# A group norm and a shifted depthwise convolution: shorter tile heads, narrower frame copies, another order around the variances

## The chip, the cores and the metric

The kernel runs on one core of a Trainium2 chip. The metric is the device time in microseconds from launch to end. An x tensor of 201 MB is read once from HBM and an output of the same size is written once.

## What is computed

`x` is (16, 768, 64, 64) in fp32. It is normalized in 32 groups of 24 channels over all pixels, per image. Each of the 48 blocks of 16 channels is then shifted by a whole number of pixels (about a multiple of 16 in each direction, up to 48), filtered with a separable 3x3 Gaussian whose centre is off by the fraction of the offset, and added to `x`:

```python
g = v.reshape(B_, G, C_ // G, H_, W_)
m = jnp.mean(g, axis=(2, 3, 4), keepdims=True)
s = jnp.var(g, axis=(2, 3, 4), keepdims=True)
gn = ((g - m) / jnp.sqrt(s + eps)).reshape(v.shape)
...
off_int = lax.stop_gradient(jnp.round(offset * SCALE)); sub = off_px - off_int
shifted = gn shifted by off_int, zero outside the image
kern = jnp.exp(-(kx * kx + ky * ky) / (2.0 * SIGMA * SIGMA)); kern = kern / kern.sum(axis=(1, 2), keepdims=True)
x = x + depthwise 3x3 convolution of shifted with kern
```

A shift of 16, 32 or 48 pixels leaves only a window of about 50, 34 or 18 rows or columns that isn't zero.

## The kernel before

**Tiles and units.** A tile is one position of the offset grid for 8 images: 16 channels x 8 images on 128 partitions, 4096 pixels each (2 MB). There are 96 tiles. Three tiles make a unit, which holds two whole groups (48 channels), so statistics are ready unit by unit: 32 units. Units go in pairs from the list `PAIRS`: an even unit is called large here (more window), an odd one small. Tiles live in `xs`, a ring of 10 slots, and are changed in place.

**SyncE** alone issues DMAs. `store(n)` waits for VectorE to be done with tile n; a load into a slot waits for the store of the tile that had it. Loads are woven in between stores in the order `EARLY` and `AGAIN`, and one waiting DMA holds back those behind it.

**TensorE** forms the group sums: 8 chunks of 512 a tile against a 0/1 matrix (in fp32 each is two passes, so 16 records a tile), all into `sum_ps` (L289). Then come `means(u + 1)` (L304 to L306), which spread ScalarE's reduced sum to the partitions, and `variances(u)` (L346 to L354), which do so with the squares. In a large unit the order is: sums of two tiles of the next unit, variances, sums of the third, means. In a small unit it is: sums of all three, variances, means. PE rows of L289 with "bands" are the first or third tile of a unit, with "halves" the second.

**ScalarE** does `sum_means` (L463), the means (L470), the squares (L484, about 3.7 us each), the variance with its scale (L492), and `fill_frame` (L417): it copies the rows of the tile that are needed, less the mean, over their whole 64 columns into the padded `frame`. There is one frame, so a copy waits for the second operation (L709) of the tile before. `fill_frame` reads a word from `fills` and picks one of four copies by the number of rows (64, 50, 34 or 18).

**GpSimd** turns the variances into the row weights `col_w`: one power for the unit (L253), then for each tile L257, L260 and L266.

**VectorE** first works out all per-tile numbers in a chain of small operations (L600 to L669), sums one tile (L677), and then runs a loop with one pass for each tile (L751, `tile_of`). A pass takes four words (kind, where to, where from, and the column of its weights) that a register load (L708) brought in during the pass before; works out registers (L727, L732); goes down four branches of `choose` (L185, L187) to one of 16 forms of `smooth_tile`, by 4 row and 4 column sizes; and issues five operations: L704 (centre and nearer neighbour in the row), L709 (the other neighbour), L713, L716 and L719 (the rows, added to x). L713 waits for `col_w`. Each operation waits for the one before it in its instruction; a gap between them of 0.04 us is what that costs.

Sizes of a tile are rows x columns, so L704 "128x3200" is a window of 50 x 64 or 64 x 50.

## Time and profile before

| | |
|---|---|
| median of 3 runs | 973.79 us (973.67 to 978.83) |
| the profiled execution | 979.06 us, its span 977.1 us |
| TensorE matmuls | 785.6 us busy, 80% |
| VectorE | 824.8 us, 84% |
| ScalarE | 638.9 us, 65% |
| GpSimd | 368.1 us, 38% |
| DMA | 98.0% of 16 engines' time in the main queue; 403.09 MB, mean 413 GB/s |
| granted TensorE clock | 0.888 |

The profile's page comes from one execution. Busy shares are means over the span. Its second part cuts the span into 40 slices of 24.4 us and gives the DMA rate of each. A group row of an engine ends with the idle time before its instructions and what ended most of it; "issue" means that nothing that the profile shows was waited for. Sequencer work (DVEq, ACTq: registers, branches) isn't counted as busy.

### The profile page before, as it was taken

Reading aid. Unit: us, or ns where it says so; the run is one execution under the profiler, and the core shown is the slowest. Engines: PE = TensorE matmul, PEld = TensorE weight load, DVE = VectorE, ACT = ScalarE, POOL = GpSimd, SP = SyncE. Lnnn points to the kernel's source line nnn. Section 1 sums busy time; section 2 is a strip of 40 time slices with the busy share of each in tenths; the row PEclk is TensorE's granted clock in tenths of the full one; section 3 lists DMA queues with packets and bytes.
Section 4 is the critical chain, followed back from the end, with each engine's and each line's share of the span. In section 5 each row is a group of like instructions: output and inputs, shape, how many; then the busy total and the mean of one; then the engine's idle time right before and its main releaser. Section 6 shows DMA issues by size and latency. Waiting matters only on the chain.

```text
span 977.1 us, 9088 instructions
## 1 busy us (share of the span) xinstructions
PE 785.6 (80%) x2132; PEld 383.6 (39%) x2132; DVE 824.8 (84%) x551; ACT 638.9 (65%) x461; POOL 368.1 (38%) x348
## 2 busy tenths in 40 slices
PE   0998987979979698897979879689797997979820
PEld 0544443434434343353434434345343443434410
DVE  7587988777798997978889899898998979797795
ACT  7778676564766747678466746577675785774661
POOL 0214034340432624013254393463845438250312
PEclk9999988989979799897998979989898897989955
DMA  9999999999999999999999999999999999999948
GB/s 364 427 401 423 392 405 429 429 429 428 430 429 430 432 428 414 430 429 430 431 429 406 398 433 376 407 419 393 431 408 430 430 427 431 431 431 430 430 208 343
DMA packets 27821, 403.09 MB, mean 413 GB/s; under 512 B 3216, under 2 KB 3216, under 8 KB 3216
## 3 DMA queue, kind: packets, MB, share of 16 engines
q1 hardware_dynamic: 27792, 402.71, 98.0%
q8 instruction: 17, 0.28, 0.1%
q14 instruction: 12, 0.10, 0.0%
HBM read 201.38 MB, written 201.33 MB: 412 GB/s over the span
## 4 chain that ended last, share of the span: by engine, by line
DVE 28%; DMA 27%; PE 20%; POOL 7%; issue 7%; ACT 5%; DVEq 3%; ACTq 2%; SPq 0%; POOLq 0%
PE sum_ps L289 17%; DMA out_dram<-xs 15%; DMA xs<-x_dram 12%; DVE xs L713 6%; DVE xs L716 6%; DVE smooth L709 6%; DVE smooth L704 6%; DVE xs L719 4%; POOL small L253 2%; POOL small L260 2%; ACT frame L417 2%; POOL small L257 2%; ACT unused L484 2%; POOL small L266 1%; ACTq L393 1%
## 5 line engine op out<-in xcount | busy, mean ns | idle before, releaser
L289 PE MATMUL sum_ps<-xs,bands 128*128 128x512 f32 x976 | 483.5, 653 | 51.2 <-DMA xs<-x_dram 51.2
L484 ACT ACTIVATE unused<-xs,small 128x4096 bf16 (+1 forms) x94 | 348.3, 3706 | 8.3 <-ACT small L470 4.8
L417 ACT ACTIVATE frame<-xs,small (+1 forms) x96 | 223.3, 2326 | 184.3 <-DVE smooth L709 183.3
L289 PEld LDWEIGHTS sum_ps<-xs,bands 128*128 128x128 f32 x976 | 200.6, 210 | 295.4 <-issue 282.2
L253 POOL TENSOR_TENSOR small<-small 128x3 f32<-128x3 f32 x32 | 41.6, 1299 | 570.6 <-ACT small L492 570.6
L289 PE MATMUL sum_ps<-xs,halves 128*128 128x512 f32 x496 | 230.0, 619 | 17.4 <-DMA xs<-x_dram 17.4
L704 DVE SCALAR_TENSOR_TENSOR smooth<-frame,side_w 128x612 f32 (+5 forms) x96 | 163.6, 1705 | 72.2 <-ACT frame L417 37.1
L713 DVE SCALAR_TENSOR_TENSOR xs<-smooth,small,xs 128x612 f32 (+5 forms) x96 | 163.5, 1703 | 51.9 <-POOL small L266 49.6
L709 DVE SCALAR_TENSOR_TENSOR smooth<-frame,side_w,smooth x96 | 159.7, 1664 | 7.5 <-DVE smooth L704 4.1
L719 DVE SCALAR_TENSOR_TENSOR xs<-smooth,small,xs 128x594 f32 (+9 forms) x96 | 159.8, 1664 | 3.4
L716 DVE SCALAR_TENSOR_TENSOR xs<-smooth,small,xs 128x594 f32 (+9 forms) x96 | 159.7, 1664 | 3.4
L289 PEld LDWEIGHTS sum_ps<-xs,halves 128*128 128x128 f32 x496 | 97.4, 199 | 146.4 <-issue 119.3
L266 POOL TENSOR_SCALAR small<-xs,small 128x3 f32<-128x3 f32 x96 | 119.5, 1245 | 9.5
L260 POOL TENSOR_SCALAR small<-small 128x1 f32<-128x1 f32 x96 | 106.6, 1110 | 8.4
L257 POOL TENSOR_SCALAR small<-small 128x1 f32<-128x1 f32 x96 | 99.7, 1039 | 3.3
L463 ACT ACTIVATE sum_ps<-sum_ps 128x512 f32<-128x512 f32 x31 | 18.0, 581 | 73.8 <-PE sum_ps L289 71.0
L304 PE MATMUL mean_ps<-small,halves 128*128 128x1 f32 x62 | 13.0, 279 | 61.6 <-ACT sum_ps L463 61.6
L304 PEld LDWEIGHTS mean_ps<-small,halves 128*128 128x128 f32 x62 | 10.7, 217 | 74.3 <-ACT sum_ps L463 74.3
L470 ACT ACTIVATE small<-mean_ps 128x3 f32<-128x3 f32 x31 | 5.4, 175 | 27.6 <-PE mean_ps L306 27.6
L492 ACT ACTIVATE small<-var_ps,small 128x3 f32<-128x3 f32 x32 | 8.2, 255 | 22.6 <-PE var_ps L354 21.7
L346 PEld LDWEIGHTS var_ps<-small,bands 128*128 128x128 f32 x62 | 11.9, 194 | 18.8 <-issue 18.8
L484 ACT ACTIVATION_READ_ACCUMULATOR unused<-xs,small 128x1 f32 x94 | 17.5, 186 | 0.0
(132 smaller groups left out, 259.3 us busy)
## 6 DMA issues: line engine op xcount, KB each, us to landing
xs<-x_dram SPq DMA_DIRECT2D x96, 2048.0 KB, 14.8
out_dram<-xs SPq DMA_DIRECT2D x96, 2048.0 KB, 17.7
smooth<-offset_dram SPq DMA_DIRECT2D x1, 48.0 KB, 4.1
```

Source lines behind the costliest of these rows:

```text
L253: V.tensor_tensor(rstd0, var, power, ALU.pow).then_inc(rstd_step, 1)
L257: V.tensor_scalar(fix[:, column], var[:, column], rstd0[:, column], rstd0[:, column], ALU.mult, ALU.mult).then_inc(rstd_step, 1)
L260: V.tensor_scalar(rstd[:, column], fix[:, column], -0.5, 1.5, ALU.mult, ALU.add).then_inc(rstd_step, 1)
L266: V.tensor_scalar(col_w[:, now * UT + i, :], base_w[:, position, :], rstd0[:, column], rstd[:, column], ALU.mult, ALU.mult).then_inc(col_w ...
L289: last = nc.tensor.matmul(sum_ps[:, :], (FIRST, SAME, SECOND)[i], slot_px(n, c * BANK, (c + 1) * BANK), start=(i == 0 and c == 0), stop=(i ...
L417: nc.scalar.activation(frame[:, bass.ds(b, rows * PITCH)].rearrange("p (r c) -> p r c", c=PITCH)[:, :, LEFT:LEFT + W], xs[:, bass.ds(a, ro ...
L484: nc.scalar.activation(unused[:, :], xs[:, bass.ds(n % SLOTS * PIX, PIX)], ACT.Square, bias=neg_mean[:, i:i + 1], accum_out=squares[:, i:i ...
L704: V.scalar_tensor_tensor(sm, frame_window(beside, cols), side_w[0][:, bass.ds(n, 1)], frame_window(src, cols), ALU.mult, ALU.add).wait_op( ...
L709: V.scalar_tensor_tensor(part, frame_window(behind, cols - 1), side_w[1][:, bass.ds(n, 1)], part, ALU.mult, ALU.add).wait_op(half_smooth, ...
L713: V.scalar_tensor_tensor(x_window(0, rows), sm, col_flat[:, bass.ds(weights + 1, 1)], x_window(0, rows), ALU.mult, ALU.add).wait_op(smooth ...
L716: V.scalar_tensor_tensor(x_window(1, rows), sm[:, 0:rows - 1], col_flat[:, bass.ds(weights, 1)], x_window(1, rows), ALU.mult, ALU.add).wai ...
L719: V.scalar_tensor_tensor(x_window(0, rows - 1), sm[:, 1:rows], col_flat[:, bass.ds(weights + 2, 1)], x_window(0, rows - 1), ALU.mult, ALU. ...
```

## The change

- A tile keeps four words, but the fourth is now the address of the nearer neighbour (`BESIDE`), worked out at setup; the column of the weights comes from the tile's number instead. `col_w` is laid out by kernel row first and tile second, and `side_w` has a column ahead, so that the count 1 to 96 indexes both. The loop runs over that count. The parity and the address `behind` are worked out in the form itself, after the first operation.
- The load of the next tile's words goes from behind the first operation to behind the second.
- `fill_frame` has six copies: the four as before, and two of 34 columns (64 or 34 rows) for tiles of 34 or 18 columns. Its word also holds a column. The words for it move into partitions 64 to 127 of `words`.
- In small units TensorE forms the variances after two tiles' sums, as in large ones. ScalarE takes the variance before `sum_means`.
- Setup has 14 more small operations on VectorE, and GpSimd six memsets fewer.

```diff
-    KIND, TO, FROM, COLUMN = range(WORDS)
+    KIND, TO, FROM, BESIDE = range(WORDS)
     ROW_BITS = (H - SIDES[-1]).bit_length()
+    NARROW = 2
+    COPIES = [(rows, W) for rows in SIDES] + [(SIDES[k], SIDES[NARROW]) for k in (0, NARROW)]
+    COL_BITS = (W - SIDES[NARROW]).bit_length()
...
+        col_w = sb("col_w", [P, 3, 2 * UT])
...
+        side_w = [sb(f"side_w{k}", [P, TILES + 1]) for k in range(2)]
         words = sb("words", [P, WORDS * (TILES + 1)], i32)
-        fills = sb("fills", [P, TILES], i32)
+        fills = words[HALF:P, 0:TILES]
...
-                    V.tensor_scalar(col_w[:, now * UT + i, :], base_w[:, position, :], rstd0[:, column],
+                    V.tensor_scalar(col_w[:, :, (now * UT + i + 1) % (2 * UT)], base_w[:, position, :], rstd0[:, column],
...
-                    early = UT if u % 2 else UT - 1
-                    sums(u + 1, range(early))
+                    sums(u + 1, range(UT - 1))
                     variances(u)
-                    sums(u + 1, range(early, UT))
+                    sums(u + 1, range(UT - 1, UT))
...
-                word = act.snap(entry, min_val=0, max_val=(len(SIDES) << ROW_BITS) - 1)
-                row = word & (1 << ROW_BITS) - 1
-                rows_kind = act.snap(word >> ROW_BITS)
+                word = act.snap(entry, min_val=0, max_val=(len(COPIES) << ROW_BITS + COL_BITS) - 1)
+                column = word & (1 << COL_BITS) - 1
+                row = (word >> COL_BITS) & (1 << ROW_BITS) - 1
+                copy_kind = act.snap(word >> ROW_BITS + COL_BITS)
                 base = act.snap(slot, min_val=0, max_val=(SLOTS - 1) * PIX)
                 first = isinstance(u, int) and u == 0 and i == 0
                 act.reg_mov(frames, u * UT + i)
-                act.reg_mov(copy_from, base + row * W)
-                act.reg_mov(copy_to, row * PITCH + PAD * PITCH)
+                act.reg_mov(copy_from, base + row * W + column)
+                act.reg_mov(copy_to, row * PITCH + column + PAD * PITCH)
+                source = act.snap(copy_from, min_val=0, max_val=SLOTS * PIX)
+                target = act.snap(copy_to, min_val=PAD * PITCH, max_val=FRAME_ROWS * PITCH)
+                done = act.snap(frames, min_val=1, max_val=TILES)
                 if i == 0:
                     act.wait_ge(fill_mean_ready, u + 1)
                 def emit(k):
-                    rows = SIDES[k]
-                    a = act.snap(copy_from, min_val=0, max_val=(SLOTS - 1) * PIX + (H - rows) * W)
-                    b = act.snap(copy_to, min_val=PAD * PITCH, max_val=(PAD + H - rows) * PITCH)
+                    rows, cols = COPIES[k]
+                    a = source.with_bounds(min_val=0, max_val=(SLOTS - 1) * PIX + (H - rows) * W + W - cols)
+                    b = target.with_bounds(min_val=PAD * PITCH, max_val=(PAD + H - rows) * PITCH + W - cols)
                     if not first:
-                        act.wait_ge(smooth_ready, act.snap(frames, min_val=1, max_val=TILES))
+                        act.wait_ge(smooth_ready, done)
                     nc.scalar.activation(
-                        frame[:, bass.ds(b, rows * PITCH)].rearrange("p (r c) -> p r c", c=PITCH)[:, :, LEFT:LEFT + W],
-                        xs[:, bass.ds(a, rows * W)].rearrange("p (r c) -> p r c", c=W),
+                        frame[:, bass.ds(b, rows * PITCH)].rearrange("p (r c) -> p r c", c=PITCH)[:, :, LEFT:LEFT + cols],
+                        xs[:, bass.ds(a, rows * W)].rearrange("p (r c) -> p r c", c=W)[:, :, 0:cols],
                         ACT.Identity, bias=fill_mean[:, i:i + 1]).then_inc(frame_ready, 1)
-                choose(act, rows_kind, 0, len(SIDES), emit)
+                choose(act, copy_kind, 0, len(COPIES), emit)
...
+                variances(u, first)
                 if ahead and not large:
                     sum_means(u + 1)
-                variances(u, first)
...
+            narrow, low, half = positive[:, :, 0], positive[:, :, 1], whole[:, :, 0]
+            chained(V.tensor_scalar(narrow, kind[:, :, 0], float(NARROW), None, ALU.is_ge))
+            chained(V.tensor_scalar(low, kind[:, :, 1], float(NARROW), float(len(SIDES)), ALU.is_ge, ALU.add))
+            chained(V.tensor_tensor(low, low, kind[:, :, 1], ALU.subtract))
+            chained(V.tensor_tensor(low, low, narrow, ALU.mult))
+            chained(V.tensor_tensor(low, low, kind[:, :, 1], ALU.add))
+            chained(V.tensor_scalar(half, kind[:, :, 1], float(NARROW), float(H - SIDES[NARROW]), ALU.is_ge, ALU.mult))
+            chained(V.tensor_scalar(half, half, float(H), None, ALU.subtract))
+            chained(V.tensor_tensor(half, half, narrow, ALU.mult))
+            chained(V.scalar_tensor_tensor(half, half, float(H), first_row[:, :, 1], ALU.add, ALU.min))
+            chained(V.scalar_tensor_tensor(code[:, :, 0], low, float(1 << ROW_BITS), half, ALU.mult, ALU.add))
+            chained(V.tensor_tensor(narrow, narrow, left, ALU.mult))
+            chained(V.tensor_scalar(narrow, narrow, float(W - SIDES[NARROW]), None, ALU.mult))
+            chained(V.scalar_tensor_tensor(code[:, :, 0], code[:, :, 0], float(1 << COL_BITS), narrow,
...
+            chained(V.tensor_tensor(code[:, :, 0], code[:, :, 0], side, ALU.subtract))
+            chained(V.tensor_scalar(by_tile(word_of[:, :, BESIDE]), for_halves(code[0:HALF, :, 0]),
...
                 dve.wait_ge(frame_ready, done)
-                V.scalar_tensor_tensor(sm, frame_window(beside, cols), side_w[0][:, bass.ds(n, 1)], frame_window(src, cols),
+                V.scalar_tensor_tensor(sm, frame_window(beside, cols), side_w[0][:, bass.ds(done, 1)], frame_window(src, cols),
                                        ALU.mult, ALU.add
                                        ).wait_op(tile_done, done_count, "sem-ge").then_inc(half_smooth, 1)
-                dve.reg_load(next_tile, words[0:1, bass.ds(done * WORDS, WORDS)])
-                V.scalar_tensor_tensor(part, frame_window(behind, cols - 1), side_w[1][:, bass.ds(n, 1)], part,
+                turn = kind_of % 2
+                behind = (src + 1 - turn).with_bounds(min_val=1, max_val=most + 1)
+                part = smooth[:, bass.ds(turn.with_bounds(min_val=0, max_val=1), rows * cols)].rearrange(
+                    "p (r c) -> p r c", c=cols)[:, :, 0:cols - 1]
+                V.scalar_tensor_tensor(part, frame_window(behind, cols - 1), side_w[1][:, bass.ds(done, 1)], part,
                                        ALU.mult, ALU.add
                                        ).wait_op(half_smooth, done_count, "sem-ge").then_inc(smooth_ready, 1)
+                dve.reg_load(next_tile, words[0:1, bass.ds(done * WORDS, WORDS)])
                 dve.wait_ge(col_w_ready, done)
-                V.scalar_tensor_tensor(x_window(0, rows), sm, col_flat[:, bass.ds(weights + 1, 1)], x_window(0, rows),
+                V.scalar_tensor_tensor(x_window(0, rows), sm, col_w[:, 0, bass.ds(done % (2 * UT), 1)], x_window(0, rows),
...
-            def tile_of(n):
-                dve.reg_mov(done_count, n + 1)
-                done = dve.snap(done_count, min_val=1, max_val=TILES)
+            def tile_of(done):
+                dve.reg_mov(done_count, done)
                 kind_of = dve.snap(next_tile[KIND], min_val=0, max_val=2 * len(SIDES) ** 2 - 1)
-                dve.reg_mov(at_turn, kind_of & 1)
-                turn = dve.snap(at_turn, min_val=0, max_val=1)
                 dst = dve.snap(next_tile[TO], min_val=0, max_val=SLOTS * PIX)
                 src = dve.snap(next_tile[FROM], min_val=1, max_val=FRAME_ROWS * PITCH)
-                dve.reg_mov(at_behind, src + 1 - turn)
-                dve.reg_mov(at_beside, src + 2 * turn - 1)
-                beside = dve.snap(at_beside, min_val=0, max_val=FRAME_ROWS * PITCH)
-                behind = dve.snap(at_behind, min_val=0, max_val=FRAME_ROWS * PITCH)
-                weights = dve.snap(next_tile[COLUMN], min_val=0, max_val=(2 * UT - 1) * 3)
+                beside = dve.snap(next_tile[BESIDE], min_val=0, max_val=FRAME_ROWS * PITCH)
...
-            with dve.Fori(0, TILES) as n:
+            with dve.Fori(1, TILES + 1) as n:
...
```

## Rows read from the trace of the kernel before

**Rows 1.** The page, part 2: DMA rate in 40 slices.
```profile
GB/s 364 427 401 423 392 405 429 429 429 428 430 429 430 432 428 414 430 429 430 431 429 406 398 433 376 407 419 393 431 408 430 430 427 431 431 431 430 430 208 343
```

**Rows 2.** Busy by stretch: PE, PEld, DVE, ACT, POOL (instructions), PEclk, DMA share, GB/s.
```profile
57.00:132.00 75.00, 67.30 (x196) 32.66 (x194) 65.37 (x41) 56.93 (x41) 22.86 (x30) 0.98 0.99 398
132.00:360.00 228.00, 194.34 (x517) 92.82 (x517) 191.18 (x113) 142.57 (x107) 75.94 (x70) 0.89 1.01 429
360.00:384.00 24.00, 21.46 (x63) 10.74 (x64) 18.33 (x18) 18.41 (x14) 9.31 (x12) 0.88 1.01 414
...
528.00:690.00 162.00, 137.16 (x374) 67.31 (x373) 147.24 (x83) 102.31 (x76) 78.94 (x52) 0.89 0.98 403
690.00:744.00 54.00, 44.33 (x124) 21.98 (x123) 49.23 (x29) 37.72 (x27) 30.15 (x19) 0.91 1.01 421
...
924.00:977.00 53.00, 9.18 (x31) 6.12 (x29) 40.43 (x28) 18.70 (x16) 15.54 (x16) 0.57 0.68 289
```

**Rows 3.** VectorE's timeline (start, length, instruction, idle before): tiles 48, 54, 60, 66, 72.
```profile
501.03 3.55 DVE L704 SCALAR_TENSOR_TENSOR smooth<-frame,side_w 128x3200 f32 x1 [0.92 <-DVE xs L719]
...
564.28 3.55 DVE L704 SCALAR_TENSOR_TENSOR smooth<-frame,side_w 128x3200 f32 x1 [0.95 <-DVE xs L719]
...
627.26 3.59 DVE L704 SCALAR_TENSOR_TENSOR smooth<-frame,side_w 128x3200 f32 x1 [0.94 <-DVE xs L719]
...
686.70 3.56 DVE L704 SCALAR_TENSOR_TENSOR smooth<-frame,side_w 128x3200 f32 x1 [1.48 <-ACT frame L417]
...
746.66 3.55 DVE L704 SCALAR_TENSOR_TENSOR smooth<-frame,side_w 128x3200 f32 x1 [1.48 <-ACT frame L417]
```

**Rows 4.** Waits of VectorE: line, releaser, us in all, times, longest.
```profile
DVE xs L713 <- POOL small L266: 49.6, 32, 5.5
DVE smooth L704 <- ACT frame L417: 37.1, 24, 5.5
...
DVE smooth L704 <- issue: 14.8, 13, 1.5
```

**Rows 5.** Chain of waits at tile 94's head (start, us, what; DVEq is the sequencer).
```profile
959.42 0.22 DVEq L727
...
959.68 0.17 DVEq L732
...
960.61 0.93 DVEq L708
```

**Rows 6.** VectorE's timeline: first operation of tile 52, third of tile 63.
```profile
549.43 1.16 DVE L704 SCALAR_TENSOR_TENSOR smooth<-frame,side_w 128x900 f32 x1 [1.18 <-issue]
...
669.20 1.42 DVE L713 SCALAR_TENSOR_TENSOR xs<-smooth,small,xs 128x1152 f32 x1 [0.67 <-POOL small L266]
```

**Rows 7.** Frame copies: ScalarE's groups by shape, and tile 52's on the timeline.
```profile
L417 ACT ACTIVATE frame<-xs,small 128x4096 f32 x12 | 45.0, 3747 | 29.8 <-DVE smooth L709 29.8
...
545.44 1.27 ACT L417 ACTIVATE frame<-xs,small  x1 [0.77 <-DVE smooth L709]
```

**Rows 8.** Timeline, unit 17: second sums, last square, the means on ScalarE.
```profile
523.35 7.03 PE L289 MATMUL sum_ps<-xs,halves 128*128 128x512 f32 x16
...
528.52 3.71 ACT L484 ACTIVATE unused<-xs,small 128x4096 bf16 x1
...
540.52 0.18 ACT L470 ACTIVATE small<-mean_ps 128x3 f32<-128x3 f32 x1 [0.83 <-PE mean_ps L306]
```

**Rows 9.** VectorE's timeline in the setup.
```profile
13.61 0.21 DVE L639 CAST fills<-smooth 128x96 int32<-128x96 f32 x1
13.86 0.21 DVE L642 SCALAR_TENSOR_TENSOR smooth<-smooth 128x48 f32<-128x48 f32 x1
...
20.33 4.42 DVE L677 TENSOR_REDUCE small<-xs 128x1 f32<-128x4096 f32 x1 [1.11 <-DMA xs<-x_dram]
```

**Rows 10.** GpSimd's timeline beside tile 48's first operation.
```profile
500.97 3.67 POOL L257 TENSOR_SCALAR small<-small 128x1 f32<-128x1 f32 x1
```

**Rows 11.** The tail: TensorE's sums of tile 94, VectorE's start of tile 95.
```profile
911.20 8.67 PE L289 MATMUL sum_ps<-xs,halves 128*128 128x512 f32 x16 [2.69 <-DMA xs<-x_dram]
...
966.19 0.56 DVE L704 SCALAR_TENSOR_TENSOR smooth<-frame,side_w 128x324 f32 x1 [1.04 <-issue]
```

**Rows 12.** TensorE's timeline: a tile's sums after an idle time.
```profile
276.94 10.04 PE L289 MATMUL sum_ps<-xs,bands 128*128 128x512 f32 x16 [6.23 <-DMA xs<-x_dram]
```

61 lines of the change are left out of this document (27 added, 34 removed).

## The prediction

> **What bounds the kernel now.** I read the page first, then the busy time by stretch, then the waits of VectorE, then the chain and the timelines around the places that these named.
>
> The page shows a DMA-bound kernel with dents. The rate stands at 427 to 433 GB/s in most of the 40 slices and falls in a few: early, around slices 22 to 29, and at the end [rows 1]. By stretches, 132 to 360 us runs at 429 GB/s and is full. I take 430 as full speed. A lost microsecond of DMA there is lost for good, since the queue is full before and after. The losses, as length times (1 - rate/430): 57 to 132 us 5.6 us, 360 to 384 us 0.9 us, 528 to 690 us 10.2 us, 690 to 744 us 1.1 us [rows 2]. The last stretch, 924 to 977 us, is the tail: all loads are in, and VectorE works off what is left.
>
> So two things can shorten the span: the 11.3 us lost in the middle (528 to 744), and the tail. In the middle VectorE sets the pace. A pair of units is 6 tiles and so 12 transfers of 2.097 MB, 58.5 us at 430 GB/s. The first operations of tiles 48, 54, 60, 66 and 72 start at 501.03, 564.28, 627.26, 686.70 and 746.66 [rows 3], so the pairs take 63.25, 62.98, 59.44 and 59.96 us: 4.7, 4.5, 0.9 and 1.4 over 58.5, together 11.5. That is the 11.3 us lost, measured a second way. VectorE's own work cannot shrink (no operation on data changes), only the idle time between its operations. That idle time is 49.6 us for row weights from GpSimd and, before a tile's first operation, 14.8 us "issue" and 37.1 us for the frame copy on ScalarE [rows 4].
>
> **The change part by part.**
>
> *Short heads.* Ahead of a tile's first operation VectorE's sequencer runs the loop's end, a block at L727 (0.22 us), one at L732 (0.17 us), and four branches [rows 5]. While the tile before is short, this isn't covered: tile 52 starts after 1.18 us of idle with "issue" as releaser, and nothing else was late [rows 6]. The change takes the parity, both derived addresses, the weights column and the n+1 out of the head. What is left is a move of the count and four names for loaded registers. The L732 block goes whole, and of L727 most: 0.17 + 0.22 and the three gaps of some 0.03 between them make 0.48; one short block stays. I take 0.43 a head. Bounds: 0 (the register work is only renamed) and 1.0 (branches get shorter too). Heads behind a tile of long operations are covered and give nothing.
>
> *The moved register load* (L708, 0.93 us [rows 5]) goes from behind the first operation to behind the second. It stalls a small tile as much in the one place as in the other, so 0. But the frame is released by the second operation, so ScalarE can copy the next one 0.2 to 0.4 us sooner after tiles of 612 elements or fewer. Parity and `behind` are now worked out during the first operation, and `done % 6` during the others: they hide behind 0.56 us at the least (0; 0.3 a small tile if not).
>
> *Narrow copies.* A frame copy of 4096 elements takes 3747 ns, one of 1152 takes 1.27 us [rows 7], so about 0.84 ns an element. Tiles with 34 or 18 columns now copy 2176 in place of 4096 or 3200 (1.6 and 0.9 us less), or 1156 in place of 2176 (0.85 less). It shortens the path only where VectorE waits for the frame. In the middle it isn't: tile 52's frame is complete at 546.7, 2.7 us before the tile starts [rows 6, 7], and the row of a large unit's first tile that does name the frame as its releaser (686.70, tile 66 [rows 3]) is of 50 columns and isn't narrowed. There it gives 0. Where it does shorten a wait, before 460 us, DMA is full and the time isn't lost now.
>
> *Variances ahead of the third tile's sums, in small (odd) units.* Before, TensorE ran 3 x 16 matmuls of the next unit, 7.03 us a tile, and then the variances. Now they come up to one tile, 7 us, sooner, and ScalarE turns them over before the means. The wait for row weights at the first tile of a small unit then goes: 0.67 us at tile 63 and again at 69 [rows 6]. At tiles 51 and 57 it is 0.40, where the variance still has to pass the frame copy on ScalarE and four GpSimd operations: I take half, 0.2. Behind the moved variances stand the third tile's sums and the next means, and behind those the squares and the frames of the small unit. The variances take 1.5 us of TensorE and no longer run beside ScalarE's sum (0.6 us), so where TensorE is late the means come about 1 us later. In unit 17 the variances would wait for the last square, which ends at 532.2; the second sums end at 530.1. So: wait 2, variance tail 0.5, third sums 7.0, ScalarE 0.7, means 0.8, makes 541, less VectorE's own lead, 540.3; before, the means came at 540.52 [rows 8]. No loss, no gain.
>
> *Setup.* 14 more chained operations on VectorE at about 0.24 us each (the spacing of L639 and L642: 13.61 and 13.86) are 3.4 us, of which 1.1 is covered by the wait of L677 for its load [rows 9]. The first unit starts 2.2 us later. Up to 57 us the DMA queue is fed by the ten first loads, so that is covered; behind it the store of tile 3 loses its margin, since it had only some 3 us of queue ahead. I charge 0.5 us. Bounds: 0 and 2.2.
>
> *GpSimd against VectorE.* GpSimd's one-element operation took 3.67 us beside a VectorE operation of 3.55 [rows 10]: it gets through at the seams. The idle heads are such seams, and they are now half as wide. The rows bound the cost: nothing, or one more of its short operations behind each large unit's second VectorE operation, some 0.35 us. I take 0 and put 0.35 a pair in the range.
> The Trainium skill (SBUF — State Buffer, "Who interferes with whom") says that a DVE instruction with two SBUF inputs holds the shared read port against a GpSimd instruction that reads SBUF, for the whole instruction. The trace agrees with that at 3.67 us. By that rule shorter heads do cost the 0.35 a pair, and the sum below would be 1.4 us less.
>
> **The sum, in the profiled run.** Up to tile 46 both kernels meet the DMA-bound chain (load, sums, means, square, frame), so nothing carries over. From there:
> - Lead at tile 48: its head and the one before, 0.8. Pair 48 to 53: heads of 52, 53 and 54, 1.3, and 0.2 of weights: 1.5. New excess 4.7 - 0.8 - 1.5 = 2.4.
> - Pair 54 to 59: the same, 4.5 - 1.5 = 3.0.
> - Pair 60 to 65: three heads 1.3, the weights 0.67, earlier release 0.2: 0.9 - 2.2 = below zero.
> - Pair 66 to 71: 1.4 - 2.4, below zero too.
> So 5.4 us are still lost in place of 11.3: gain 5.9. The dent at 360 to 384 (0.9) comes from the same lateness of tile 32, which leads by 0.7: half, 0.4. Tail: its start hangs on the load that TensorE takes at 911.20, and in the last large unit the order is as before; then the heads of 91, 94 and 95 (0.25 and twice 0.43; tile 95's shows 1.04 us of "issue") [rows 11]: 1.1. In all 5.9 + 0.4 + 1.1 - 0.5 = 6.9 us.
>
> The profiled execution took 979.06 us, its span 977.1; the median of the three runs is 973.79, 5.3 below it, so either it was a slow one or the profile costs something. I take the gain off the median: **966.9 us**.
>
> **The rivals.**
> 1. *Nothing in the middle.* Something else sits just under the heads: the frame after the square (545.44 for tile 52, four microseconds ahead of its use), or the weights. Then only the tail's 1.1 and the 0.67s count: 972.5. Against it: "issue" is the last releaser of these heads [rows 6]. Chance 0.18.
> 2. *The heads don't shrink.* Copies of registers stay, or six copy kinds and longer leaves bring later code. Then 0.2 to 0.67 a pair from the weights, less the setup: 973.3. Chance 0.08.
> 3. *The middle is mended whole.* A head loses 0.9: four a pair make 3.6, and 63.25 - 0.8 - 3.8 is at 58.5. Then 11.3 + 0.9 + 2.0 - 0.5 go: 960.1. Chance 0.12.
> 4. *Slower: TensorE now waits for squares.* Place: variances of units 17, 19, 21 and 23, ahead of the third sums. The sums after an idle TensorE took 10.04 us in place of 7.03 [rows 8, 12]. If the new wait brings that about, the means come 3 us later; the square and the frame of tile 52 have 0.8 us of slack, so VectorE starts 2.2 us later in each of four pairs and in the two that follow. The middle loses 5.4 + 4 x 2.2 + 2 x 1 = 16 in place of 11.3 and the start 2.2: with the tail's 1.1 off, 979.6. It decides from about 1 us of delay of the means. Against it: the wait in unit 17 is only 2 us, and TensorE had just worked for 16 us. Chance 0.10.
> The Trainium skill (TensorE: Matmul & The Clock Gate, Part 1) has the array fall to 1.2 GHz after an idle time and return to 2.4 only under work. The granted clock of 0.57 in the tail [rows 2] and the 10.04 us agree. It is the rule that speaks for rival 4.
>
> **How the numbers follow.** Forecast 0.52 at 966.9; the rivals 0.18, 0.08, 0.12 and 0.10. The forecast's own bounds: heads 0.25 to 0.7, ports 0 to 1.4, start 0 to 2.2, give 962.5 to 971. The range takes in rivals 1 and 2 and stops near rival 3: 960.5 to 974.5. About 0.5% (4.9 us) is what a measurement can tell from no change, so "faster" is below 968.9: 0.38 of the forecast's and 0.12 of rival 3's chance, 0.50. Slower, above 978.7: 0.09. The rest, 0.41, is the same.
>
> **What would show each step.** The idle time before tile 52's first operation falls from 1.18 to about 0.75 us; the L732 block is gone. The frame copies of 4096 elements fall from 12 to 4 (the tiles of 50 columns). The wait for row weights falls below 30 us from 49.6. The rate in 528 to 690 us rises from 403 to about 415 GB/s, and first operations of tiles 48, 54 and 60 stand 61 to 62 us apart. TensorE shows a gap of about 2 us ahead of the variances in unit 17. The prediction is wrong if the heads are as wide as before, if the sums after the variances take 9 us or more, or if tile 52 waits for its frame.

## The result and the profile after

| | before | after |
|---|---|---|
| median, 20 runs each, in turns | 977.11 us (973.67 to 979.31) | 972.45 us (970.14 to 976.21) |
| ratio after/before | | 0.9961, 95% interval 0.9951 to 0.9972 |
| profiled execution, its span | 979.06, 977.1 us | 973.67, 971.6 us |
| GpSimd busy | 368.1 us | 436.9 us |
| frame copies, mean of 96 | 2326 ns | 1909 ns |

The change gains 3.8 us by the ratio (2.7 to 4.8), 4.7 by the medians. The forecast was 966.9, a gain of 6.9. The time lies inside the range (960.5 to 974.5), and the outcome is within 0.5% of no change, to which I gave 0.41. The direction was right, the size wasn't. The forecast missed the median by 5.5 us: 3.3 of them are the median that it started from (973.79 where the twenty runs give 977.11), 2.2 the gain.

The page of the kernel after, DMA rate in 40 slices, where [rows 1] has that of before:

```profile
GB/s 361 429 396 396 401 400 431 429 428 430 429 432 430 428 430 429 431 427 431 428 429 428 405 431 407 411 430 409 430 431 431 431 431 430 431 431 428 424 206 346
```

Counted from 1, the dents of slices 16 and 22 (414, 406) are gone (429, 428), and slices 25, 26, 28 and 30 (376, 407, 393, 408) read 407, 411, 409 and 431. But the early ones, 3 to 6, are worse on the whole: 396, 396, 401, 400 where there were 401, 423, 392, 405.

Busy by stretch of the kernel after (PE, PEld, DVE, ACT, POOL with instructions, then granted clock, DMA share, GB/s), beside [rows 2]:

```profile
57.00:132.00 75.00, 70.22 (x201) 33.75 (x199) 67.90 (x42) 53.12 (x41) 36.72 (x30) 0.98 0.99 391
132.00:360.00 228.00, 190.43 (x518) 91.18 (x519) 191.68 (x113) 136.14 (x106) 93.74 (x72) 0.92 1.01 429
360.00:384.00 24.00, 21.03 (x60) 10.05 (x59) 18.84 (x18) 16.89 (x15) 10.38 (x13) 0.92 1.01 431
528.00:690.00 162.00, 137.57 (x379) 66.06 (x377) 151.68 (x85) 98.53 (x77) 90.25 (x56) 0.94 1.00 417
690.00:744.00 54.00, 46.09 (x128) 22.50 (x129) 50.66 (x30) 33.18 (x25) 31.47 (x17) 0.91 1.01 430
```

By the measure of the prediction, length times (1 - rate/430): 528 to 690 loses 4.9 us in place of 10.2, 690 to 744 nothing in place of 1.1, 360 to 384 nothing in place of 0.9. So 7.3 us are gained, and 57 to 132 loses 6.8 in place of 5.6.

Waits of VectorE in the kernel after (line, releaser, us in all, times, longest), beside [rows 4]:

```profile
DVE smooth L727 <- ACT frame L423: 69.3, 30, 6.9
DVE xs L740 <- POOL col_w L270: 29.2, 26, 5.2
DVE smooth L727 <- DVE xs L746: 11.0, 27, 0.6
DVE xs L740 <- DVE smooth L734: 5.4, 12, 1.0
```

(L727, L734, L740, L743 and L746 are the five operations that were L704, L709, L713, L716 and L719.) "issue" is gone as a releaser. The wait for row weights fell by 20.4 us, and the wait for the frame rose by 32.2.

VectorE's timeline in the kernel after at tiles 52, 54, 60 and 63, beside [rows 3, 6]:

```profile
546.97 1.16 DVE L727 SCALAR_TENSOR_TENSOR smooth<-frame,side_w 128x900 f32 x1 [0.64 <-ACT frame L423]
...
560.75 3.55 DVE L727 SCALAR_TENSOR_TENSOR smooth<-frame,side_w 128x3200 f32 x1 [0.41 <-DVE xs L746]
...
622.12 3.55 DVE L727 SCALAR_TENSOR_TENSOR smooth<-frame,side_w 128x3200 f32 x1 [0.41 <-DVE xs L746]
...
663.63 1.42 DVE L740 SCALAR_TENSOR_TENSOR xs<-smooth,col_w,xs 128x1152 f32 x1 [0.45 <-POOL col_w L270]
```

Heads (the idle time before a tile's first operation) of 1.18, 0.95 and 0.94 us are 0.64, 0.41 and 0.41 us long: 0.54 less each. Tile 48 starts at 499.37, so the first two pairs take 61.38 and 61.37 us where they took 63.25 and 62.98.

**A ledger of the queue.** To compare executions I counted, for each kernel, when the main DMA queue had finished its k-th transfer of 2 MB, less k times 4.865 us (what one takes when the queue is full). The rise of that figure between two points is DMA time lost there.

```
transfers done (at about)     before  before, again  after
25  (126 us)                  10.7    9.1            12.4
101 (496 us)                  13.2    12.5           14.2
106 (520 us)                  13.3    12.5           14.2
146 (715 us)                  25.3    23.0           19.7
185 (905 us)                  26.0    23.6           20.6
192 (the end)                 41.9    39.5           36.5
```

Middle (106 to 146): 12.0 and 10.5 before, 5.5 after. Up to 25 transfers the kernel after loses 1.7 us more than the first execution of the kernel before and 3.3 more than the second. From 185 transfers to the end the figure rises by 15.9 us in all three, so by this measure the tail is no shorter. The second column is a second execution of the kernel before, which the experiments below brought.

### The profile page after: what moved, and what is told of

It is laid out like the page before. It is cut to its first block, busy times and chain, and to the rows that moved or that the text cites. A ratio compares the mean times of both kernels' runs of the same rounds, so it can differ in the third digit from the quotient of the medians.

```text
span 971.6 us, 9186 instructions
## 1 busy us (share of the span) xinstructions
PE 776.9 (80%) x2132; PEld 375.9 (39%) x2132; DVE 827.7 (85%) x565; ACT 598.0 (62%) x461; POOL 436.9 (45%) x342
## 4 chain that ended last, share of the span: by engine, by line
DMA 36%; DVE 29%; PE 15%; POOL 7%; issue 5%; ACT 3%; ACTq 2%; DVEq 1%; SPq 0%; POOLq 0%
DMA out_dram<-xs 21%; DMA xs<-x_dram 14%; PE sum_ps L293 13%; DVE xs L740 7%; DVE xs L743 6%; DVE xs L746 5%; DVE smooth L727 5%; DVE smooth L734 4%; POOL small L261 3%; POOL small L264 2%; POOL small L257 2%; ACT frame L423 1%; ACT unused L490 1%; ACTq L395 1%; POOL col_w L270 1%
## 5 line engine op out<-in xcount | busy, mean ns | idle before, releaser
L423 ACT ACTIVATE frame<-xs,small (+1 forms) x96 | 183.3, 1909 | 178.6 <-DVE smooth L734 176.1
L257 POOL TENSOR_TENSOR small<-small 128x3 f32<-128x3 f32 x32 | 51.6, 1612 | 497.2 <-ACT small L498 497.2
L293 PE MATMUL sum_ps<-xs,halves 128*128 128x512 f32 x496 | 221.8, 600 | 21.5 <-DMA xs<-x_dram 21.5
L727 DVE SCALAR_TENSOR_TENSOR smooth<-frame,side_w 128x612 f32 (+5 forms) x96 | 163.6, 1704 | 82.1 <-ACT frame L423 69.3
L740 DVE SCALAR_TENSOR_TENSOR xs<-smooth,col_w,xs 128x612 f32 (+5 forms) x96 | 163.6, 1704 | 37.5 <-POOL col_w L270 29.2
L734 DVE SCALAR_TENSOR_TENSOR smooth<-frame,side_w,smooth x96 | 159.8, 1665 | 3.4
L743 DVE SCALAR_TENSOR_TENSOR xs<-smooth,col_w,xs 128x594 f32 (+9 forms) x96 | 159.8, 1665 | 3.4
L746 DVE SCALAR_TENSOR_TENSOR xs<-smooth,col_w,xs 128x594 f32 (+9 forms) x96 | 159.8, 1664 | 3.4
L293 PEld LDWEIGHTS sum_ps<-xs,halves 128*128 128x128 f32 x496 | 94.0, 192 | 146.5 <-issue 113.2
L264 POOL TENSOR_SCALAR small<-small 128x1 f32<-128x1 f32 x96 | 134.3, 1399 | 8.4
L270 POOL TENSOR_SCALAR col_w<-xs,small 128x3 f32<-128x3 f32 x96 | 126.1, 1313 | 9.5
L261 POOL TENSOR_SCALAR small<-small 128x1 f32<-128x1 f32 x96 | 124.4, 1296 | 3.3
```

The costliest lines, as they stand in the source:

```text
L257: V.tensor_tensor(rstd0, var, power, ALU.pow).then_inc(rstd_step, 1)
L261: V.tensor_scalar(fix[:, column], var[:, column], rstd0[:, column], rstd0[:, column], ALU.mult, ALU.mult).then_inc(rstd_step, 1)
L264: V.tensor_scalar(rstd[:, column], fix[:, column], -0.5, 1.5, ALU.mult, ALU.add).then_inc(rstd_step, 1)
L270: V.tensor_scalar(col_w[:, :, (now * UT + i + 1) % (2 * UT)], base_w[:, position, :], rstd0[:, column], rstd[:, column], ALU.mult, ALU.mul ...
L293: last = nc.tensor.matmul(sum_ps[:, :], (FIRST, SAME, SECOND)[i], slot_px(n, c * BANK, (c + 1) * BANK), start=(i == 0 and c == 0), stop=(i ...
L423: nc.scalar.activation(frame[:, bass.ds(b, rows * PITCH)].rearrange("p (r c) -> p r c", c=PITCH)[:, :, LEFT:LEFT + cols], xs[:, bass.ds(a, ...
```

## The experiments

Each time is a median, and each ratio is to the kernel before, run beside it. That had 976.13 us beside the first four experiments; 976.35 beside the kernel before again, nine moves, 14 setup operations and the shorter chain; 977.11 beside four moves, the old heads, 42 setup operations and the last one.

**Heads alone.** The kernel after, with copies of 64 columns and the old order put back, so that mainly what concerns VectorE's heads is left of the change. Twelve of the 14 setup operations go with the narrow copies (not shown in this excerpt), and the first tile starts at 30.57 us, as before the change, where the kernel after has 32.58.

```diff
-    COPIES = [(rows, W) for rows in SIDES] + [(SIDES[k], SIDES[NARROW]) for k in (0, NARROW)]
-    COL_BITS = (W - SIDES[NARROW]).bit_length()
+    COPIES = [(rows, W) for rows in SIDES]
+    COL_BITS = 0
...
-                    sums(u + 1, range(UT - 1))
+                    early = UT if u % 2 else UT - 1
+                    sums(u + 1, range(early))
```

> The kernel before with the short heads and the four words alone: all copies are 64 columns wide and the variances of small units stay behind the third sums. Theory A (the heads carry the gain): heads such as tile 52's fall from 1.18 to 0.64 us, pairs of units in 501 to 690 us take about 61.5 us of VectorE's time, the middle loses 5 to 7 us of DMA in place of 12, and the time is 4 to 6 us below before (971 to 973 where before is 977). Theory B (the new order carries it, heads hit another wait): the middle still loses 10 us or more, time within 2 us of before.

972.84 us, ratio 0.996 (0.9945 to 0.9974): the gain of the whole change. The middle loses 7.2 us by the ledger, a little over what theory A had.

**Order alone.** The kernel before with the new order on TensorE and ScalarE.

```diff
-                    early = UT if u % 2 else UT - 1
-                    sums(u + 1, range(early))
+                    sums(u + 1, range(UT - 1))
                     variances(u)
-                    sums(u + 1, range(early, UT))
+                    sums(u + 1, range(UT - 1, UT))
...
+                variances(u, first)
                 if ahead and not large:
                     sum_means(u + 1)
-                variances(u, first)
```

> The kernel before with only the order around the variances changed in small units, on TensorE and ScalarE. Theory A: waits for row weights at the first tile of a small unit fall, but the second tile waits for its frame in their place, since the means come about 1 us later; the middle keeps 10 to 12 us of loss; time within 1.5 us of before. Theory B: the time falls by 3 us or more.

977.52 us, ratio 1.002 (1.0006 to 1.0034): it gains nothing, and costs 2.0 us (0.6 to 3.3). VectorE's waits in this run:

```profile
DVE smooth L702 <- ACT frame L416: 66.1, 30, 7.3
DVE xs L711 <- POOL small L266: 19.5, 22, 5.1
```

The waits for weights fell from 49.6 to 19.5 us, those for the frame rose from 37.1 to 66.1 [rows 4]. Together they are 85.6 us in place of 86.7: the order renames the wait. In the program's new order the means, on which the squares and the frames of a small unit hang, stand behind the variances.

**Old order in the kernel after** (the two edits above, backwards).

> The changed kernel with the order around the variances put back. Theory A: within 1.5 us of the changed kernel (972), either way; if the order costs, it is by the frames of tiles 4, 76, 82 and 88, which wait up to 6.9 us. Theory B: back near before, 976 to 977.

972.77 us, ratio 0.9962 (0.9948 to 0.9976), like the kernel after. Against heads alone this adds the narrow copies and the twelve setup operations that work out their words: 972.84 and 972.77. The two together bring nothing. Each by itself isn't separated: if the operations cost here what they cost in the kernel before (below), the copies would have gained as much, and no run tells.

**The weights table later in the setup.** In the kernel after, VectorE's sum of its own tile comes before the chain that works out the row weights' table.

```diff
+            dve.wait_ge(loaded[UT - 1], 16)
+            V.tensor_reduce(own_sum, slot_px(UT - 1), mybir.AxisListType.X, ALU.add).then_inc(vector_sum_ready, 1)
...
             dve.wait_ge(exps_ready, 1)
             chained(V.tensor_tensor(norm[:, :, :], e[:, 0], e[:, 1], ALU.add))
```

> The changed kernel; on VectorE the last part of the setup (norms, side weights, base weights; some 3.4 us) now runs behind the sum of the third tile instead of ahead of it. Theory A (the longer setup costs 1.7 us at the start, seen as lost DMA up to 126 us): L677's successor starts at about 20.3 again, the loss up to 126 us falls from 12.4 to about 10.5, time 1.5 to 2 us below the changed kernel: about 970.5. Rival: the loss there is one of SyncE's order of stores and loads and isn't moved by VectorE; time as the changed kernel's.

972.88 us, ratio 0.9959 (0.9944 to 0.9974): no gain shown. VectorE's first tile starts at 30.51 in place of 32.58 and 57 to 90 us runs at 400 GB/s in place of 384 (1.2 us), but 90 to 132 us at 389 in place of 397 (0.8 us the other way). I had expected 1.5 to 2 us; an interval 3 us wide doesn't rule out 1.2, but there is no sign of them.

**The kernel before again.**

> The kernel before, unchanged, profiled a second time: it prices the spread of a single execution, which my sums were read from. My theory: part of what missed in the size is that the gain read from one profiled execution (span 977.1, a long one) was taken off a median of three that lay below the twenty runs that followed (973.79 against 977.11). Then the ratio is 1.000 with its interval around it, the span of this profile may lie anywhere from 973 to 978, and the middle (528 to 690 us) again runs at 401 to 408 GB/s, with tiles 48, 54 and 60 62.7 to 63.4 us apart. The rival: the execution that I read was of the usual kind, in which case the span is 976.5 to 977.5 again and the stretches agree within 1 GB/s.

976.78 us, ratio 1.0006 (0.9991 to 1.002), span 974.7. Stretches 57 to 132 and 528 to 690:

```profile
57.00:132.00 75.00, 67.19 (x196) 32.66 (x194) 64.86 (x40) 57.98 (x42) 25.53 (x30) 0.98 1.00 408
...
528.00:690.00 162.00, 140.57 (x373) 68.14 (x371) 147.01 (x84) 100.12 (x74) 81.27 (x53) 0.88 0.99 407
```

The same program: 408 against 398 GB/s in the one stretch and 407 against 403 in the other [rows 2]. The execution that I read was 2.4 us longer than this one, of which 1.5 in the middle, while the median from which I took the gain was the lowest of all: 973.79 of 3 runs against 976.1 to 977.1 of 17 to 25. The first theory holds.

**Longer heads, nine moves.** The kernel before with

```diff
                 dve.reg_mov(done_count, n + 1)
+                for k in range(9):
+                    dve.reg_mov(at_turn, n + k + 2)
```

> The kernel before with nine more moves of a register in the head of a tile. Theory (heads carry the gain): each head behind a short tile grows by about 0.5 us (an estimate from the block of L732, 0.17 us for about three register instructions), tile 52's from 1.18 to about 1.7, and the time goes the other way by as much as the short heads brought, some 4 to 6 us: 980.5 to 982.5 beside 976.5, ratio 1.004 to 1.006. Stretch 528 to 690 falls from 403 to about 392 GB/s. Rival (the time is set by the rest of the tile loop or by fixed things, and heads_only gained by something else, such as fewer instructions to fetch): ratio within 1.001 of the kernel before.

993.64 us, ratio 1.0182 (1.0162 to 1.0202). The direction holds, the size doesn't: 17.3 us, three times what I expected. Tile 52's head, the waits, and the stretches that lost most:

```profile
554.22 1.16 DVE L704 SCALAR_TENSOR_TENSOR smooth<-frame,side_w 128x900 f32 x1 [1.80 <-issue]
```
```profile
DVE smooth L704 <- issue: 91.7, 53, 6.7
DVE xs L713 <- POOL small L266: 18.2, 18, 4.3
```
```profile
360.00:384.00 24.00, 20.93 (x52) 9.82 (x51) 18.37 (x17) 17.46 (x11) 9.17 (x9) 0.86 0.96 377
384.00:528.00 144.00, 121.67 (x307) 57.66 (x306) 124.07 (x67) 94.39 (x65) 58.40 (x50) 0.87 1.01 423
528.00:690.00 162.00, 134.47 (x365) 66.63 (x363) 143.37 (x79) 100.59 (x73) 76.63 (x51) 0.87 0.96 393
690.00:744.00 54.00, 46.03 (x116) 22.46 (x117) 48.00 (x25) 35.42 (x25) 32.38 (x19) 0.84 0.98 399
```

The head is 0.62 us longer, much as the short ones are shorter, and it is about so in the other tiles whose head was open before (tile 53 from 1.01 to 1.64, tile 69 from 0.66 to 1.28). Only tile 0 starts 1.2 us later (31.72 against 30.48). That speaks against stalls at some tiles as the cause. But now stretches lose that were full: 384 to 528 us runs at 423 GB/s (2.3 us lost), 690 to 744 loses 3.9 in place of 1.1. "issue" is the releaser of 53 heads in place of 13.

**Longer heads, four moves** (as above, `range(4)`).

> The kernel before with four more moves in the head in place of nine: tile 52's head should go from 1.18 to about 1.45 us (0.61 for nine moves makes 0.07 a move). Heads 0.54 shorter brought 3.5 to 4.5 us, heads 0.61 longer cost 17.3. Theory (thresholds: a pair of units loses DMA time only for what it is over 58.5 us, and each lengthening brings more pairs over): the cost of this step lies between, and below half of 17.3: about 6 us, 982 to 983, ratio 1.005 to 1.007. Rival (something else comes with nine moves, such as a fetch of instructions that no longer fits, and heads cost in proportion): less than 3 us, or nearly the whole 17.

981.31 us, ratio 1.0045 (1.003 to 1.0061): 4.2 us, a little under the 6 of the theory, and a quarter of the price of nine moves; tile 52's head is 1.48 us. With heads alone, and the kernel before as the zero, there are four points: 0.54 us shorter, 3.9 us gained; 0.30 longer, 4.2 lost; 0.62 longer, 17.3 lost. In proportion to four moves, nine would cost 8.7. So the cost grows faster than the heads, and of the rival's two prices neither came.

The thresholds are one reason: the pairs from tiles 42, 72 and 78 took 58.73, 58.04 and 58.20 us before, 58.93, 58.58 and 59.03 with four moves and 59.81, 59.53 and 58.99 with nine, so pairs that had been near or under 58.5 went over it. The waits are another, which I hadn't named. In this run

```profile
DVE xs L713 <- POOL small L266: 32.8, 23, 6.9
```

where there were 49.6 us: when a tile starts later, it waits less for its row weights. At tiles 48, 51, 54, 57 and 60 that wait was 0.39 to 0.67 us and is gone with four moves. The pair from tile 48 went from 63.25 to 63.42 us with four moves and to 64.92 with nine. How much of the 17.3 us each of the two makes isn't separated.

**The old heads in the kernel after.**

```diff
+                for k in range(8):
+                    dve.reg_mov(done_count, done + k + 1)
                 dve.reg_mov(done_count, done)
```

> The changed kernel with eight moves in the head, which gives back the 0.54 us that its heads had lost (tile 52's head from 0.64 to about 1.18), and leaves the narrow copies, the new order and the setup. Theory (the short heads carry the whole gain, narrow copies and order nothing): the time of the kernel before or 1 to 2 us over it, 976.5 to 978.5, ratio 1.000 to 1.002, stretch 528 to 690 us at 402 to 408 GB/s. Rival (order and narrow copies bring a part on their own): 973 to 975.

977.59 us, ratio 1.0009 (0.9996 to 1.0022), 528 to 690 us at 407 GB/s:

```profile
547.29 1.16 DVE L727 SCALAR_TENSOR_TENSOR smooth<-frame,side_w 128x900 f32 x1 [1.20 <-issue]
```

With the heads at 1.20 us again, the rest of the change leaves the time of the kernel before. Shown from both sides (this run and heads alone): the short heads carry the gain. Order, narrow copies and longer setup come to about nothing together.

**A longer setup.** The kernel before with 14, and then with 42 more chained operations ahead of the weights table:

```diff
+            for _ in range(14):
+                chained(V.tensor_scalar(code[:, :, 0], code[:, :, 0], 1.0, None, ALU.mult))
             dve.wait_ge(exps_ready, 1)
```

> The kernel before with 14 more chained one-column operations in VectorE's setup, which is what the change adds there by my count. My prediction charged 0.5 us with bounds of 0 and 2.2; the ledger of the kernel after against before showed 1.7 us more DMA loss by 126 us. If the setup is the cause of that: the ledger at 126 us rises by 1 to 2 us over the run of the kernel before of this call, and the time by the same, 977.5 to 978.5. Rival (that 1.7 us was the spread of single executions, and the first ten loads cover the setup): the time is within 0.5 us of the kernel before.

> The kernel before with 42 more chained operations in the setup, three times the dose of the run with 14, which came out 2.1 us slower (0.4 to 3.3). At 0.24 us each they are 10.1 us. Theory (the setup lies on the path, of which only about 1 us is covered): 976.4 plus 8 to 9 us, 984 to 986, with the ledger of the DMA queue up by as much by 126 us. Rival (the first ten loads cover the setup and the 2.1 us were spread): up to 978.5.

978.41 us, ratio 1.0019 (1.0004 to 1.0034), and 983.19 us, ratio 1.0064 (1.0048 to 1.008): 2.1 us by the medians (0.4 to 3.3 by the ratio) for 3.4 us of operations and 6.1 (4.7 to 7.8) for 10.1, so some 0.6 us a microsecond; for the large dose I had expected 8 to 9. VectorE's first tile starts at 32.65 and 38.86 where it started at 30.55. Stretch 57 to 90 us, with no more operations, 14 and 42:

```profile
57.00:90.00 33.00, 30.83 (x96) 15.60 (x95) 28.28 (x20) 26.74 (x20) 8.71 (x11) 0.97 0.99 405
```
```profile
57.00:90.00 33.00, 30.82 (x96) 15.43 (x94) 29.08 (x19) 27.50 (x21) 7.95 (x10) 0.99 0.95 376
```
```profile
57.00:90.00 33.00, 33.00 (x93) 15.83 (x92) 29.28 (x18) 27.62 (x19) 7.94 (x10) 1.00 0.79 321
```

The ledger at ten transfers (53.5 us) is 4.8 to 4.9 us in all of them, so the first loads cover the setup up to there, as predicted. Behind them 405, 376 and 321 GB/s are 1.9, 4.1 and 8.4 us lost. Up to 126 us the small dose no longer stands out: its ledger has 10.6 us there, where the two executions of the kernel before have 10.7 and 9.1, and the large dose has 15.9. So the price of 14 operations rests on the times of the runs, that of 42 on the queue as well.

**A shorter chain on GpSimd.** The kernel after, with the power and one multiplication a tile.

```diff
-                    V.tensor_scalar(fix[:, column], var[:, column], rstd0[:, column], rstd0[:, column],
-                                    ALU.mult, ALU.mult).then_inc(rstd_step, 1)
...
-                    V.tensor_scalar(rstd[:, column], fix[:, column], -0.5, 1.5,
-                                    ALU.mult, ALU.add).then_inc(rstd_step, 1)
...
-                                    rstd[:, column], ALU.mult, ALU.mult).then_inc(col_w_ready, 1)
+                                    None, ALU.mult).then_inc(col_w_ready, 1)
```

> The changed kernel with a shorter chain on GpSimd: the power and then one multiplication a tile. It leaves out the refinement step of the reciprocal root. Theory: in the kernel after, GpSimd finds narrower seams between VectorE's operations, and so the third operation of each large unit's first tile waits 0.72 to 1.17 us for its row weights where it waited 0.39 to 0.67. That is a cost of the short heads that my sum took at nothing. With a third of the GpSimd operations these waits go to 0 to 0.2: in the middle 4 x 0.7 = 2.8 us of VectorE's time, of which the stretch from 528 to 690 us can give back 2 to 2.8, and in the tail the sums of the last but one unit are followed by VectorE's third operation 1 to 2 us sooner. Together 3 to 4.5 us below the kernel after: 968 to 969.5, ratio 0.991 to 0.993 to the kernel before, stretch 528 to 690 us at 422 to 425 GB/s. Rival (the frames or the heads are late next, so the waits only change their name): 971.5 to 973, ratio 0.995 to 0.997, and the frame waits grow by what the weights waits lose.

971.56 us, ratio 0.9943 (0.9922 to 0.9965), 528 to 690 us at 418 GB/s. The waits for weights at tiles 48, 54, 60 and 66 are gone (0.72 to 0.04), but tile 52 says where the time went:

```profile
547.72 1.16 DVE L717 SCALAR_TENSOR_TENSOR smooth<-frame,side_w 128x900 f32 x1 [1.38 <-ACT frame L413]
```

It waits 1.38 us for its frame in place of 0.64. The pair takes 61.4 us as before; the next two take 60.7 and 56.6 in place of 61.4 and 57.8. Over the whole kernel the waits for weights fell from 29.2 to 12.4 us and those for the frame rose from 69.3 to 87.7. So the rival holds for the first pair and for the sum of the waits, the theory for the next two pairs; the time lies nearer to the rival, and its interval overlaps that of the kernel after.

**Three edits together.** The kernel after with the old order, the late weights table and the shorter chain on GpSimd (the refinement step is left out here too).

> The changed kernel with the order of before on TensorE and ScalarE, the weights table worked out behind the first unit's own sums, and the short chain on GpSimd. It leaves out the refinement step of the reciprocal root. Each of the three alone gave 971.6 to 972.9 beside 972.45, so none showed a gain of its own over 1 us. Theory (the order of before frees the frame of tile 52 from the late means, and only then do the shorter weights waits count): 968.5 to 970.5, ratio 0.992 to 0.994. Rival (what is left is the floor: VectorE's five operations a tile are 59.1 us in pair 48 to 53 where the queue has 58.5): 971 to 972.5, ratio 0.995 and up.

969.45 us, ratio 0.9922 (0.99 to 0.9945). Tile 52 and the stretch from 528 to 690 us:

```profile
545.70 1.16 DVE L718 SCALAR_TENSOR_TENSOR smooth<-frame,side_w 128x900 f32 x1 [0.64 <-DVE xs L737]
```
```profile
528.00:690.00 162.00, 137.82 (x381) 67.15 (x379) 153.40 (x85) 99.39 (x79) 44.91 (x24) 0.91 1.01 422
```

With the old order the frame is there in time again, and pairs 48 and 54 both take 60.7 us. It is faster than both kernels, at the price of the step that it leaves out. The intervals of this run and of the shorter chain alone overlap, so what the order and the table add to the shorter chain is likely, not shown.

## Why the prediction was right and wrong

**What bounds the kernel: right.** The time follows the losses of the queue, and the middle is VectorE's: heads shorter and longer by 0.3 to 0.6 us moved both.

**Heads: right, a little low.** 0.43 us expected, 0.54 measured.

**The middle: right, with some luck in its parts.** I had the pairs at 63.25 - 1.5 and 62.98 - 1.5; they took 61.38 and 61.37 us. Expected were 5.4 us still lost; the ledger has 5.5. In the pair from tile 54 the three heads gave 0.3 us more than I took and the moved variances 0.2 more (tile 57's wait of 0.39 is gone, I had halved it), while the wait for weights at tile 54 grew by 0.33, which I had at 0. Rival 3 (mended whole) failed on what VectorE does: in the fastest kernel here, with almost no waits there, the pair from tile 48 still takes 60.7 us against 58.5.

The gain by the ledger, term by term (us; minus is a loss):

```
                              expected  against before  against before, again
start, to 25 transfers          -0.5        -1.7             -3.3
25 to 106 (dent at 360)          0.4         0.8              1.6
106 to 146 (the middle)          5.9         6.5              5.0
146 to the end (the tail)        1.1        -0.2             -0.3
sum                              6.9         5.4              3.0
```

Three steps failed.

**The base: the largest part of the miss.** "I take the gain off the median." That median, 973.79 of three runs, lay 3.3 us below the one of twenty, 977.11: 3.3 of the 5.5 us by which the forecast was off. And the loss of the middle was read from a long execution (12.0 us; 10.5 in the second, 10.6 and 10.2 in those with a longer setup, whose middle is the same). I had seen that execution and median were 5.3 us apart and drew nothing from it. Against 977.11 the same 6.9 us would have read 970.2. With 10.8 us as the usual loss the middle gains 5.3.

**The setup: mis-sized.** "I charge 0.5 us. Bounds: 0 and 2.2." The change starts its first tile 2.1 us later (32.58 against 30.48), as worked out. I had written that the store of tile 3 had only some 3 us of queue ahead and then charged less than a quarter of the delay, with no row for that share. In the kernel before, 14 operations cost 2.1 us (0.4 to 3.3) and 42 cost 6.1. What they cost inside the kernel after is not shown: the late table, which gives the first tile its 2.1 us back, gained nothing, and heads alone, which does without twelve of them, isn't faster than the whole change. The ledger has 1.7 or 3.3 us lost at the start where I had 0.5, and the setup is the likely cause of a part.
One more loss there stays open. Stretch 90 to 132 us ran at 388 to 416 GB/s in the six kernels with short heads (397 on average) and at 392 to 418 in the eight executions with old or longer heads (410): 1.3 us, which the late table didn't give back (389). The old order in the kernel after had 416 there, but 377 in the stretch before it where the kernel after has 384; with the shorter chain and the late table beside it, it had 388. No run here tells what shorter heads do to the queue at that point, and the spread inside each set is wider than the difference.

**The tail: right for VectorE, not in the time.** From tile 90's first operation to the end of VectorE's last took 51.86 us, 50.86 in the second execution, and 49.78 after: 1.1 less than the latter, as expected. The 51.86 holds a wait of 2.10 us for weights at tile 90 where the second had 1.11. But the ledger shows none of it: from 146 transfers to the end the kernel after loses 16.8 us where the two executions of the kernel before lost 16.6 and 16.5. The queue is 5.4 us ahead of the execution that I read at 185 transfers, and tile 90 starts only 3.9 us earlier, behind a wait for its frame of 2.04 us in place of 1.60; tile 88 waited 6.42 us for its frame, where its head had been 0.89. Heads alone, with tile 88 at 0.36, loses 15.9 from 146 on, the old order in the kernel after 16.5, so the order may have a part in it; why the 1.1 us didn't arrive stays open.

**The moved register load: right at 0.** Tile 95 waited 0.69 us behind its first operation and now 0.71 behind its second:

```profile
960.19 0.55 DVE L727 SCALAR_TENSOR_TENSOR smooth<-frame,side_w 128x324 f32 x1 [0.51 <-DVE xs L746]
960.78 0.54 DVE L734 SCALAR_TENSOR_TENSOR smooth<-frame,side_w,smooth  x1
962.03 0.56 DVE L740 SCALAR_TENSOR_TENSOR xs<-smooth,col_w,xs 128x324 f32 x1 [0.71 <-DVE smooth L734]
```

**Narrow copies: 0 as far as can be seen** (their own effect isn't separated from that of their setup operations), and 4 copies of 4096 elements in place of 12.

**The variances' place: half right.** Tile 63's wait for weights fell from 0.67 to 0.45 and not to 0, tile 51's from 0.40 to 0.08. Tile 57's went from 0.39 to nothing. TensorE's gap of 2 us in unit 17 wasn't there. TensorE in the kernel after, from the second sums on:

```profile
524.29 7.03 PE L293 MATMUL sum_ps<-xs,halves 128*128 128x512 f32 x16
531.16 0.28 PE L350 MATMUL var_ps<-small,bands 128*128 128x1 f32 x2
...
532.64 7.11 PE L293 MATMUL sum_ps<-xs,bands 128*128 128x512 f32 x16
```

The last square had ended at 529.9, sooner than I assumed, so the variances follow at once, and the sums behind them take 7.11 us: rival 4's mechanism didn't start. But the other half of its chain did: the means came at 541.46, 0.9 us later than before in a stretch that started 1.7 us earlier, and tile 52's head now names the frame as its releaser, which I had put down as a sign of being wrong. The frame is complete at 546.76, 0.21 us before the tile starts, and with heads alone the head is 0.64 us long without it. That is rival 1's mechanism (the frame just under the head), at its edge. It costs nothing at 0.64 us of head, and 0.7 us as soon as something else gets faster, as the shorter chain on GpSimd showed.

**GpSimd's seams: the bound was the value in two pairs of four.** I took 0, with 0.35 us a pair in the range. The wait at the first tile went from 0.39 to 0.72 us in the pairs from 54 and 60, but only from 0.67 to 0.73 and 0.72 in those from 48 and 66: 0.8 us in all. Tile 54 in the kernel after:

```profile
560.75 3.55 DVE L727 SCALAR_TENSOR_TENSOR smooth<-frame,side_w 128x3200 f32 x1 [0.41 <-DVE xs L746]
564.34 3.50 DVE L734 SCALAR_TENSOR_TENSOR smooth<-frame,side_w,smooth  x1
568.56 3.55 DVE L740 SCALAR_TENSOR_TENSOR xs<-smooth,col_w,xs 128x3200 f32 x1 [0.72 <-POOL col_w L270]
```
```profile
559.48 1.58 POOL L257 TENSOR_TENSOR small<-small 128x3 f32<-128x3 f32 x1 [11.30 <-ACT small L498]
561.16 3.36 POOL L261 TENSOR_SCALAR small<-small 128x1 f32<-128x1 f32 x1
564.61 3.28 POOL L264 TENSOR_SCALAR small<-small 128x1 f32<-128x1 f32 x1
567.99 0.35 POOL L270 TENSOR_SCALAR col_w<-xs,small 128x3 f32<-128x3 f32 x1
```

And GpSimd at the same tile before:

```profile
562.47 1.58 POOL L253 TENSOR_TENSOR small<-small 128x3 f32<-128x3 f32 x1 [13.29 <-ACT small L492]
564.15 0.34 POOL L257 TENSOR_SCALAR small<-small 128x1 f32<-128x1 f32 x1
564.58 3.30 POOL L260 TENSOR_SCALAR small<-small 128x1 f32<-128x1 f32 x1
```

Before, the power ended 0.23 us ahead of VectorE's first operation (564.28) and the next one-column operation still began in the gap, at 0.34 us. Now the power ends 0.31 us behind that start (560.75), the next one takes 3.36 us, and the chain ends in the gap behind VectorE's second operation: 0.72 us of wait in place of 0.39. This costs 0.33 us in the pair. GpSimd's busy time of 436.9 us in place of 368.1 looks like more of the same, and mostly isn't: it is 383.2 us with the heads alone, 425.2 with the order alone and 425.9 with the old heads put back in the kernel after. The kernel before had 374.8 us in its second execution, so the narrower gaps make 8 to 15 us and the order most of the rest. That the order does it by letting GpSimd's chain start beside VectorE's longer operations is my reading; the time of the kernel doesn't follow it.
The Trainium skill (SBUF — State Buffer, "Who interferes with whom") has a DVE instruction with two SBUF inputs hold the shared read port against a GpSimd instruction that reads SBUF, for its whole length. The trace agrees, with 3.36 us beside VectorE's 3.55.

## What to carry to other kernels

Take the price of a term and the time that it is taken off from the same set of runs, and read two executions where they lie 5 us apart. Where a queue is full in most of a kernel, a microsecond on the engine that feeds it has no one price: here heads 0.54 us shorter brought 3.9 us (heads alone), 0.62 us longer cost 17.3. When two experiments differ in more than the part that they are named for, as the narrow copies and their setup did here, say so before reading the difference. An edit that moves a wait from one producer to another (here weights for frames) should be costed as the sum of both waits.

## What the runs showed of the hardware

- A register move in VectorE's head costs some 0.07 us (nine make 0.62, four 0.30). Four of them in each of 96 passes cost 4.2 us of a 977 us kernel, nine 17.3.
- One GpSimd operation on 128x1 takes 0.34 us in a gap of VectorE and 3.28 to 3.67 us beside its operations of 3.5 us. With the order alone changed, no operation added, its busy time went from 368.1 (374.8 in a second execution) to 425.2 us.
- The same program differed by 10 GB/s in one stretch of 75 us (398 and 408) and by 2.4 us in its span, from one execution to the next.
